# Values of four streams in three tiles, outputs a pair later and new orders in a chain of attention layers

## The reference

```python
xn = rmsnorm(x, norm_w)
q, k, v = xn @ wq, cond @ wk, cond @ wv
attn = softmax(einsum('btgrd,bsgd->bgrts', qg, k) / sqrt(8))
x = x + (einsum('bgrts,bsgd->btgrd', attn, v) @ wo)
q, k, v = x @ Wq, ctx @ Wk, ctx @ Wv
probs = softmax(q @ k.T / 8 + col_bias)
x = (probs @ v) @ Wo + bo + x
```

## Time and profile before

| | |
|---|---|
| median of 3 runs | 2015.4 us |
| the profiled execution: time, span | 2012.08 us, 2010.3 us |
| mean granted TensorE clock | 0.973 |
| busy: TensorE, VectorE, GpSimd, ScalarE | 94%, 83%, 75%, 72% |
| DMA queue 1 | 1,164,412 packets, 305.43 MB, 81.1% of 16 engines |
| chain that ended last | PE 63%, DMA 11%, POOL 9%, issue 6%, SPq 4%, DVE 4%, ACT 2% |

### The profile page before, as it was taken

One profiled execution on the slowest core, in us unless ns is written; L12 is line 12 of the kernel. 1 busy time (PEld: TensorE's weight loads), 2 busy tenths in 40 slices (PEclk: granted clock), 3 DMA queues, 4 the chain that ended last, 5 costly groups with the idle time before them and its releaser, 6 DMA issues.

```text
span 2010.3 us, 76315 instructions
## 1 busy us (share of the span) xinstructions
PE 1886.1 (94%) x28784; PEld 1570.3 (78%) x28784; DVE 1672.3 (83%) x3516; ACT 1443.4 (72%) x2603; POOL 1497.9 (75%) x1830
## 2 busy tenths in 40 slices
PE   5699999999899998999999999999989999999995
PEld 5578887788788887888778887888878788888874
DVE  7588888898788887888788888889878888898873
ACT  3377777777677776777677777777767777777762
POOL 2478777787687876788777887778767787788862
PEclk7599999999999999999999999999999999999997
DMA  4278888989889899898888888888887888787884
GB/s 157 55 141 161 160 160 159 166 159 159 150 162 163 156 166 148 164 165 155 161 152 167 159 156 154 171 162 159 157 151 161 161 159 159 154 162 162 162 149 102
DMA packets 1164823, 310.79 MB, mean 155 GB/s; under 512 B 1139254, under 2 KB 1163132, under 8 KB 1164412
## 3 DMA queue, kind: packets, MB, share of 16 engines
q1 hardware_dynamic: 1164412, 305.43, 81.1%
HBM read 15.93 MB, written 4.19 MB: 10 GB/s over the span
## 4 chain that ended last, share of the span: by engine, by line
PE 63%; DMA 11%; POOL 9%; issue 6%; SPq 4%; DVE 4%; ACT 2%; POOLq 0%; ACTq 0%; DVEq 0%
PE ring L1129 35%; DMA arena<-arena 10%; PE sc L1262 6%; PE o_ps L1129 6%; PE ring L1331 4%; PE o_ps L1280 3%; POOL arena L589 3%; PE sc L1245 2%; PE sc L1260 2%; POOL p_sm L566 2%; DMA arena<-p_sm 2%; SPq L443 2%; POOL v_packed L584 1%; POOL p_sg L561 1%; PE ring L1200 1%
## 5 line engine op out<-in xcount | busy, mean ns | idle before, releaser
L561 POOL TENSOR_TENSOR p_sg<-arena,p_sg 128x512 f16<-128x512 f32 (+1 forms) x256 | 347.5, 1357 | 205.9 <-ACT p_sg L626 205.9
L1129 PE MATMUL ring<-ctx_two,m_w 128*128 128x154 f16 x6144 | 442.8, 232 | 2.2 <-DVE o_tg L818 2.2
L1129 PEld LDWEIGHTS ring<-ctx_two,m_w 128*128 128x128 f16 x6144 | 426.2, 98 | 3.2 <-DVE o_tg L818 3.1
L1001 DVE TENSOR_TENSOR arena<-sc,row_max 128x616 f32<-128x616 f32 (+2 forms) x512 | 405.7, 793 | 17.4
L566 POOL TENSOR_TENSOR p_sm<-arena,p_sm 128x616 f16<-128x616 f32 x256 | 337.6, 1319 | 99.7 <-ACT p_sm L626 99.7
L1129 PE MATMUL ring<-wv_m,ctx_two 128*77 128x512 f16 x1536 | 363.1, 381 | 1.0 <-DVE q_mix L822 1.0
L626 ACT ACTIVATE arena<-ring 128x462 f16<-128x462 f32 (+1 forms) x384 | 196.6, 512 | 141.7 <-PE ring L1129 141.7
L589 POOL TENSOR_TENSOR arena<-arena 128x1024 f16<-128x1024 f32 x128 | 272.9, 2132 | 29.1 <-ACT arena L626 25.4
L1129 PEld LDWEIGHTS ring<-wv_m,ctx_two 128*77 128x77 f16 x1536 | 165.2, 116 | 149.1 <-DVE q_mix L822 46.6
L1262 PE MATMUL sc<-arena,x_s 128*128 128x512 f16 (+1 forms) x1152 | 263.4, 337 | 0.0
L720 ACT ACTIVATE arena<-arena,log_w,rstd 128x512 f32<-128x512 f32 (+1 forms) x256 | 227.4, 888 | 9.2 <-DVE arena L1001 9.2
(11 more groups left out here) (160 smaller groups left out, 3611.6 us busy)
## 6 DMA issues: line engine op xcount, KB each, us to landing
ctx_nat<-in_ctx_dram SPq DMA_DIRECT2D x64, 77.0 KB
x_nat<-in_x_dram SPq DMA_DIRECT2D x64, 64.0 KB, 2.9
arena<-p_sg SPq DMA_TRANSPOSE x256, 3.3
arena<-p_sm SPq DMA_TRANSPOSE x256, 3.9
out_dram<-y_out SPq DMA_DIRECT2D x64, 64.0 KB, 2.2
arena<-in_L_xattn_Wk_dram SPq DMA_DIRECT2D x2, 1024.0 KB, 6.0
arena<-in_L_xattn_Wv_dram SPq DMA_DIRECT2D x2, 1024.0 KB, 6.5
arena<-arena SPq DMA_TRANSPOSE x128, 4.7
```

The source lines that it names most:

```text
L561: pool.tensor_tensor(p_sg[k][:, LO, 0:e - a], probs_flat[:, a:e], p_sg[k][:, HI, 0:e - a], ALU.subtract).then_inc(sems["pg_lo"], 1)
L1001: dve.tensor_tensor(shifted[:, hs, :], s_view[:, hs, :], row_max[:, hs].unsqueeze(2).to_broadcast([P, hs.stop - hs.start, S]), ALU.subtrac ...
L1129: ins = pe.matmul(out, a, b, start=(n == 0), stop=(n == len(passes) - 1))
```

## The change

- **Values.** The 77 rows of the fourth stream of each four (stream 3 or 7, "part 3") are cut into pieces of 26, 26 and 25. `ctx_four` has room for 26 more context columns behind each stream's 77, and `context_parts` (GpSimd) copies the pieces there. `context_values` of the first three streams makes 103 or 102 rows at once; part 3 runs no `context_values` and no `values` on ScalarE or VectorE. Its rows are copied from the three tiles into `v_fourth` by SP (`move_values`, one DMA per stream), and `values_m` of part 3 waits for them.
- **GQA output product.** `wo_g` and `o_tg` are fp32: ScalarE copies the turned outputs once (`turned`), `low_turned` goes, and `output_g` is one fp32 matmul.
- **Maxima.** Two parts, heads 0 to 12 and 13 to 15, in place of 6, 7 and 3; the first waits for the second score bank.
- **Outputs.** `turn_out(m - 4)`, `output_m(m - 6)` and `finish_m` or `last_layer(m - 6)` take the place of m - 2 and m - 4: one pair later.
- **Orders.** SP and TensorE are in the diff. GpSimd: `x_parts(g+2)`, `inverse_norm`, `low_part(g)` twice, `spread_keys`, `pack_values`, `context_parts`, `x_parts(m+2)`, `low_part(m, 0)`, `low_out`, `low_part(m, 1)`. ScalarE: `folded` three times, `exponential_g` 0, `turn_context`, `high_g` 0, `exponential_g` 1, `last_layer`, `high_g` 1, `keys_values`, `queries`, `picked_values`, `exponential_m` 0, `high_m` 0, `values` 0, `turned`, `high_out`, `values` 1, `exponential_m` 1, `high_m` 1. VectorE: `maximum_g`, `folded` 0 and 1, `shift_g` 0, `first_x`, `folded` 2, `shift_g` 1, `turn_context`, `normalise_g`, `finish_m`, `finish_g`, `maximum_m` 0, `shift_m` 0, `keys_values`, `queries`, `normalise_m` twice, `maximum_m` 1, `shift_m` 1, `values` twice.

The diff, without the counts of semaphores and the lists of GpSimd, ScalarE and VectorE:

```diff
-    MAX_PARTS = list(zip((0, BANK // S, 2 * BANK // S), (BANK // S, 2 * BANK // S, H)))
+    MAX_PARTS = [(0, 2 * BANK // S), (2 * BANK // S, H)]
...
+    PART = -(-S // 3)
+    PART_OF = [(i * PART, min(S, (i + 1) * PART)) for i in range(3)]
+    def part(m):
+        return stream(m) % 4
+    def rows(m):
+        a, e = PART_OF[part(m)]
+        return S + e - a
+    def same_tile_before(m):
+        return m - (8 if part(m) == 1 else 4)
+    def split_stream(m):
+        return m - PLACES[layer(m)] + 2 * (3 - part(m))
...
-        uses = [("g", lead, k) for k in chunks] + [("yg", g - 4, 0), ("ct", g + 4, 0), ("ym", m - 4, 0), ("kv", g + 2, 0)]
-        return uses + [("vp", g, 0), ("q", g + 2, 0), ("ot", g - 2, 0), ("v", m, 0), ("v", m, 1)]
+        return [("g", lead, chunks[0]), ("g", lead, chunks[1]), ("g", lead, chunks[2]), ("ct", g + 4, 0), ("ym", m - 6, 0),
+                ("yg", g - 4, 0), ("kv", g + 2, 0), ("vp", g, 0), ("q", g + 2, 0), ("ot", g - 2, 0),
+                ("v", m, 0), ("v", m, 1)]
...
-        ctx_two = [sb(f"ctx_two{n}", [P, 2, KC, 2, S], F16) for n in range(STREAMS // 2)]
-        ctx_t = [ctx_two[n // 2][:, :, :, n % 2, :] for n in range(STREAMS)]
+        ctx_four = [sb(f"ctx_four{n}", [P, 2, KC, 4, S + PART], F16) for n in range(STREAMS // 4)]
+        ctx_t = [ctx_four[n // 4][:, :, :, n % 4, 0:S] for n in range(STREAMS)]
...
-        v_mha = [sb(f"v_mha{n}", [P, 2, H, MD + 1], F16) for n in range(2)]
+        v_tile = [sb(f"v_tile{n}", [P, 2, H, MD + 1], F16) for n in range(2)]
+        v_fourth = sb("v_fourth", [P, 2, H, MD + 1], F16)
+        v_mha = [v_tile[0], v_tile[1], v_tile[0], v_fourth]
...
+            def move_values(it, m):
+                a, e = PART_OF[part(m)]
+                sp.wait_ge(sems["v_lo"], at("v_lo", it, m, 2))
+                sp.nop(nofuse=True)
+                fourth = m - 2 * (part(m) + 1)
+                if exists(it, fourth):
+                    sp.wait_ge(sems["om_raw"], at("om_raw", it, fourth, 2))
+                    sp.nop(nofuse=True)
+                moved = m - (2 if part(m) else 4)
+                if exists(it, moved):
+                    sp.wait_ge(sems["v_moved"], at("v_moved", it, moved, 16))
+                    sp.nop(nofuse=True)
+                sp.dma_start(v_fourth[a:e].rearrange("p a h d -> p (a h d)"),
+                             v_mha[part(m)][S:S + e - a].rearrange("p a h d -> p (a h d)")).then_inc(sems["v_moved"], 16)
...
             def pair(it, n):
+                if exists(it, m - 2) and part(m - 2) != 3:
+                    move_values(it, m - 2)
+                if exists(it, m - 4):
+                    turn_out(it, m - 4)
                 if exists(it, g):
                     turn_g(it, g, 0)
                     turn_g(it, g, 1)
+                if layer(g + 4) == 0 and exists(it, g + 4) and exists(it + 1, g + 4):
+                    load(it, g + 4)
+                if layer(m - 6) == LAYERS - 1 and exists(it, m - 6):
+                    store(it, m - 6)
                 if exists(it, m):
                     turn_m(it, m, 0)
-                if layer(m - 4) == LAYERS - 1 and exists(it, m - 4):
-                    store(it, m - 4)
-                if layer(g + 4) == 0 and exists(it, g + 4) and exists(it + 1, g + 4):
-                    load(it, g + 4)
-                if exists(it, m - 2):
-                    turn_out(it, m - 2)
-                if exists(it, m):
...
+            def context_parts(it, g):
+                c = ctx_four[stream(g) // 4]
+                pool.wait_ge(sems["ct_lo"], at("ct_lo", it, g, 1))
+                for n, (a, e) in enumerate(PART_OF):
+                    piece = c[:, :, :, 3, a:e].rearrange("p a k s -> p (a k) s")
+                    ins = pool.tensor_tensor(c[:, :, :, n, S:S + e - a].rearrange("p a k s -> p (a k) s"), piece,
+                                             ones_h[:, :].unsqueeze(2).to_broadcast([P, 2 * KC, e - a]), ALU.mult)
+                ins.then_inc(sems["ct_parts"], 1)
...
             def values(it, n, m, k):
-                if k == 0 and exists(it, m - 4):
-                    act.wait_ge(sems["om_raw"], at("om_raw", it, m - 4, 2))
-                high(v_mha[m // 2 % 2][0:S, HI, n0 // MD:n1 // MD, 0:MD], ring[0:S, b, :].rearrange("p (h d) -> p h d", d=MD),
+                before, r = same_tile_before(m), rows(m)
+                if k == 0 and exists(it, before):
+                    act.wait_ge(sems["om_raw"], at("om_raw", it, before, 2))
+                    act.wait_ge(sems["v_moved"], at("v_moved", it, before, 16))
+                high(v_mha[part(m)][0:r, HI, n0 // MD:n1 // MD, 0:MD], ring[0:r, b, :].rearrange("p (h d) -> p h d", d=MD),
...
-            def high_turned(it, n, g):
+            def turned(it, n, g):
...
-                high(o_tg[:, HI, :], ring[:, b, 0:T], 1.0).then_inc(sems["ot_hi"], 1)
+                high(o_tg[:, :], ring[:, b, 0:T], 1.0).then_inc(sems["ot_copy"], 1)
...
             def maximum_m(it, m, k):
-                dve.wait_ge(sems["sm_raw"], at("sm_raw", it, m, k + 1))
+                dve.wait_ge(sems["sm_raw"], at("sm_raw", it, m, k + 2))
...
-            def low_turned(it, n, g):
-                b = ring_bank(n, ("ot", g, 0))
-                dve.wait_ge(sems["ot_hi"], at("ot_hi", it, g, 1))
-                low(o_tg[:, LO, :], ring[:, b, 0:T], 1.0, o_tg[:, HI, :]).then_inc(sems["ot_lo"], 1)
...
             def folded(it, n, m, k):
-                ct, w, b, (h0, h1) = ctx_two[stream(m) // 2], layer(m) // 2, bank_for(it, n, ("g", m, k)), G_CHUNKS[k]
+                two = slice(stream(m) % 4, stream(m) % 4 + 2)
+                ct, w, b, (h0, h1) = ctx_four[stream(m) // 4], layer(m) // 2, bank_for(it, n, ("g", m, k)), G_CHUNKS[k]
...
-                    ins = split_product(ring[:, b, (h - h0) * 2 * S:(h - h0 + 1) * 2 * S],
+                    ins = split_product(ring[:, b, (h - h0) * 2 * S:(h - h0 + 1) * 2 * S].rearrange("p (t s) -> p t s", t=2),
...
-                                          hl(lambda i: ct[:, i, kc].rearrange("p t s -> p (t s)"))) for kc in range(KC)])
+                                          hl(lambda i: ct[:, i, kc, two, 0:S])) for kc in range(KC)])
...
             def context_values(it, n, m, k):
-                ct, w, b, (n0, n1) = ctx_t[stream(m)], layer(m) // 2, bank_for(it, n, ("v", m, k)), V_CHUNKS[k]
-                split_product(ring[0:S, b, :],
-                              [(hl(lambda i: ct[:, i, kc, :]), hl(lambda i: wv_m[w][:, i, kc, n0:n1])) for kc in range(KC)]).then_inc(sems["v_raw"], 1)
+                w, b, (n0, n1), r = layer(m) // 2, bank_for(it, n, ("v", m, k)), V_CHUNKS[k], rows(m)
+                ct = ctx_four[stream(m) // 4][:, :, :, part(m), :]
+                if k == 0:
+                    pe.wait_ge(sems["ct_parts"], at("ct_parts", it, split_stream(m), 1))
+                split_product(ring[0:r, b, :],
+                              [(hl(lambda i: ct[:, i, kc, 0:r]), hl(lambda i: wv_m[w][:, i, kc, n0:n1])) for kc in range(KC)]).then_inc(sems["v_raw"], 1)
...
-                pe.wait_ge(sems["v_lo"], at("v_lo", it, m, 2))
+                if part(m) != 3:
+                    pe.wait_ge(sems["v_lo"], at("v_lo", it, m, 2))
+                else:
+                    pe.wait_ge(sems["v_moved"], at("v_moved", it, m - 2, 16))
...
-                                            [(hl(lambda i: p_tm[:, k, i, h - k * HALF, :]), hl(lambda i: v_mha[m // 2 % 2][:, i, h, :]))])
+                                            [(hl(lambda i: p_tm[:, k, i, h - k * HALF, :]), hl(lambda i: v_mha[part(m)][:, i, h, :]))])
...
             def output_g(it, n, g):
-                pe.wait_ge(sems["ot_lo"], at("ot_lo", it, g, 1))
-                split_product(ring[:, b, 0:T], [(hl(lambda i: wo_g[w][:, i, :]), hl(lambda i: o_tg[:, i, :]))]).then_inc(sems["yg_raw"], 1)
+                pe.wait_ge(sems["ot_copy"], at("ot_copy", it, g, 1))
+                pe.matmul(ring[:, b, 0:T], wo_g[w][:, :], o_tg[:, :], start=True, stop=True).then_inc(sems["yg_raw"], 1)
...
             def pair(it, n):
+                if exists(it, lead):
+                    folded(it, n, lead, chunks[0])
                 if exists(it, g):
                     scores_g(it, g)
                 if exists(it, lead):
-                    folded(it, n, lead, chunks[0])
                     folded(it, n, lead, chunks[1])
                     folded(it, n, lead, chunks[2])
                 if exists(it, g - 2):
                     values_g(it, g - 2)
+                if layer(g + 4) == 0 and exists(it, g + 4):
+                    turn_inputs(it, n, g + 4)
+                if exists(it, m - 6):
+                    output_m(it, n, m - 6)
                 if exists(it, m):
                     scores_m(it, m, 0)
                 if exists(it, g - 4):
                     output_g(it, n, g - 4)
-                if layer(g + 4) == 0 and exists(it, g + 4):
-                    turn_inputs(it, n, g + 4)
```

(11 more changed lines are left out.)

113 lines of the change are left out of this document (60 added, 53 removed).

## The result

The changed kernel took 2045.3 us (median of 4 runs, 2033.5 to 2052.0), the kernel before 2014.0 beside it (4 runs, 2012.3 to 2023.8): ratio 1.0138, interval 1.0088 to 1.0188. That is slower, where 1958 us was forecast, and outside the range of 1889 to 2004. The profiled execution took 2033.5 us, so 12 us less than the median.

What follows compares the result with a forecast made beforehand. The prediction took TensorE to bound quiet pairs (13.94 us), with stalls of 12.1 us a round, mostly for transposed outputs. Its terms summed as 2012.1 + 5 - 13 - 46 = 1958 us, range 1889 to 2004.

Steps and rivals of the forecast that it cites:

- Outputs one pair later, -46: `turn_out` issued a pair earlier than it is read: TensorE's wait in `output_m` goes, 46 us less, bounds 0 and -59.
- Output product in fp32, +5: `output_g`: one fp32 matmul for three fp16 adds 0.05 us a pair, 5 us in 96 pairs, up to 9.
- Maxima in two parts, slack in VectorE (rival 4): VectorE starts 1.1 us later, after the second score bank; in a normal pair 0.9 us of slack covers it.
- rival 4: VectorE's loop becomes the bound in every pair, slower: 2051 us at a path of 14.6 us; chance 0.10.
- the turn of the loop: Between rounds: a 2.9 us gap without releaser, 4.7 us a round with its pair and slow matmuls.
- Part-3 pairs at 13.5 instead of 13.94, -13: Pairs without values are bound by the path to the turned outputs' copy: 0.4 us shorter, 32 times, 13 us less.
- rival 2: The clock falls in each part-3 pair's gap: 1.25 us, 32 times, +40, giving 1998 us; chance 0.14.
- the row at 547.52: TensorE wait in the earlier trace, cited against rival 2: after 2.26 us idle, 24 matmuls took 1.50 us.
- the rule of the Trainium skill: On TensorE's clock: short matmul bursts with idle waits between let it fall each time; by it, 1998 us.
- Rival 3: Output wait only replaced, by `turn_m` held behind the moved transpose and the values copy: 2004 us; chance 0.09.
- The forecast's case: Whole kernel: three of four quiet pairs at 14.0 us, one at 13.5, `output_m` wait gone: 1958 us; chance 0.52.

Runs made afterwards that it cites:

- e15_late_early_product: Kernel before with outputs one pair later, their transpose first in the queue's list, `output_m` ahead of the first MHA scores, two `o_s`: 1974.7 us, ratio 0.9783.
- e2_four_values: Changed kernel with the sharing undone, all four streams making their own values by matmuls: 1976.2 us, ratio 0.9798.
- e10_four_two_os: Changed kernel with all four streams' values made by matmuls and two `o_s` buffers: 1974.9 us, ratio 0.9802.
- e11_filled_two_os_no_copy: Changed kernel with unread matmuls filling the part-3 gap, two `o_s` and no copies of values (streams 3 and 7 left out): 1980.9 us, ratio 0.9821.
- e4_norm_first: Changed kernel with GpSimd's `inverse_norm` ahead of `x_parts(g+2)` again, as before the change: 2038.5 us, ratio 1.0120.
- e3_no_copy: Changed kernel without `move_values` and the waits for it, values of streams 3 and 7 left out: 2019.8 us, ratio 1.0011.
- e1_two_os: Changed kernel with two `o_s` buffers in turn for the output's parts: 2029.0 us, ratio 1.0066.
- e9_filled_two_os: Changed kernel with six unread matmuls in the part-3 pairs and two `o_s` buffers: 2005.5 us, ratio 0.9950.

## Why the prediction was wrong

**Outputs one pair later, -46.** Right: -44 in `e15_late_early_product`. That it is right rests on `output_m` being moved ahead of the scores, which the prediction used ("may start when `output_m` of the pair has freed `o_t`") but did not price; with `output_m` left where it was, the kernel took 158 us more with the transpose at the head of the list, and 571 more with it at the end and two `o_s`.

**Output product in fp32, +5.** Right in size by TensorE's busy time in `output_g`: 49.3 us for 128 items in `e2_four_values`, against 42.3 before, so 0.055 each and 7 in all. In the time it does not show (1974.9 and 1974.7 us for `e10_four_two_os`, which has it, and `e15_late_early_product`, which has not), and the length of a pair does not give it either: a quiet pair takes 14.03 us with it and 13.93 before, but in the looped rounds of `e15_late_early_product`, with the old product, it takes 14.03 too.

**Maxima in two parts, slack in VectorE (rival 4).** Right that it is covered: nearly all pairs of `e2_four_values` take 14.0 to 14.6 us, with TensorE busy throughout, except those about the turn of the loop.

**Part-3 pairs at 13.5 instead of 13.94, -13.** This is the step that failed: the sharing, put at -13 us, measured +69 (3.40 points, `e2_four_values`). The path of the pair itself was read rightly: with the three disturbances away, the quiet part-3 pair of each looped round takes 13.49 us (`e11_filled_two_os_no_copy`), and in the changed kernel TensorE stands idle for 1.90 in front of the folded product (2.2 forecast), released by ScalarE's `o_tg`. But there only the last of the eight rounds has 13.49 at this place. The step costed the pair by that one path, let the next pair be a quiet one, and put the clock, the queue and the buffers at nothing. In fact the two together take 1.3 to 2.8 us more than forecast, in the looped rounds mostly in the first, in the last round in the second. Three prices were missing:
- *The clock behind the gap*, 1.06 points, 21 us. This was rival 2, at +40 and 0.14. Its mechanism holds: filling the gap with unread matmuls removes the falls and the time. Its size was off, since it had the clock fall in all 32 pairs, at 1.25 us each; it fell behind 13 of 31 gaps, at 1.6 us (14, 22 and 23 in `e4_norm_first`, `e3_no_copy` and `e1_two_os`, with gaps as long). The forecast set the row at 547.52 against it (2.26 us idle, clock kept); that row was one draw of a thing that goes either way. The prediction took the rule of the Trainium skill (page "TensorE: Matmul & The Clock Gate", section "HAM oscillation — how this bites in real kernels") to mean a fall in every part-3 pair. The page's case is another one: there each burst of matmuls is shorter than the wait behind it, and here a gap of 1.90 us stands behind some 11.5 us of matmuls. The traces alone decide, with a fall behind some of the gaps.
- *The one `o_s`*, 0.72 points, 15 us. No rival had it. With `turn_out` of an item issued a pair later, `o_s` is held until then, and the next `high_out` waits for that transpose, 52 times. The prediction asked what frees `o_t`, which `turn_out` writes, and never what `turn_out` reads and from then on holds longer. The later `turn_out` alone doesn't bring the wait: without copies it is 4.6 us (`e3_no_copy`) and without the sharing 3.0 (`e2_four_values`), against 58.2. It is a second price of the copies.
- *The copies*, 1.27 points, 26 us. The step said "anything from nothing to the longest landing seen, 6.32 us, is hidden". That counts when the copy lands and it was true; no wait of TensorE in the changed kernel is put down to `v_fourth`. It left out what is queued behind: "I cost the queue at nothing, and it would cost about 1 us where a transpose is held up". Rival 3 had this wait, at the price of the output's gain and a chance of 0.09; the output's gain was kept and the wait came on top.

Together 3.17 points by `e11_filled_two_os_no_copy`, 64 us. From the forecast's 1958 to the measured 2045 are 87.

**The rest, 23 us,** is still in `e11_filled_two_os_no_copy` (1981 against 1958). A quiet part-3 pair is 13.49 us there and the pair behind it 14.03, as forecast:

```profile
1831.88:1845.37 13.49, 12.88 (x216) 11.03 (x216) 11.55 (x23) 10.09 (x18) 11.19 (x15) 1.00 1.04 167
1845.37:1859.40 14.03, 14.03 (x224) 12.02 (x223) 11.90 (x24) 10.75 (x20) 11.74 (x15) 1.00 1.09 155
```

What is longer is the turn of the loop. Its gap without releaser, 2.92 us before in the turn of the earlier trace rows, is in this kernel (total of 5 turns, longest 6.7):

```profile
PE ring L1188 <- issue: 29.6, 5, 6.7
```

5.9 us a turn, where the kernel before has 14.3 us in five: 15 us more. The forecast had carried the turn over unchanged. In the changed kernel it is two gaps a turn, 21.1 us in all. The remaining 8 us or so are not accounted for; among them, not every part-3 pair of this kernel gains: the four of a looped round take 14.57, 14.40, 13.49 and 14.05 us in the mean, against 14.59, 14.31, 14.01 and 14.55 with four values products (`e2_four_values`). Why the gap grows is open: the profile names no releaser, and no run was made for it. It is short where pairs are full of work (16.0 in `e2_four_values`) and in `e9_filled_two_os`, so neither the new order of the program nor the filling alone explains it.

**The chances.** The forecast's case had 0.52 and its gain of 57 us consisted for four fifths of a term that came true. The range ended at 2004 because each rival was counted alone: rivals 2 and 3 both came true in part, in the part-3 pairs and those behind them, beside a cost that no rival listed. Their common root, a queue and two engines with little slack around a pair made irregular, was one case that needed a chance of its own on the slow side.

## What to carry to other kernels

When a change makes every fourth pass of a pipeline lighter, the pass may gain little, and it and the next one can lose more: cost both, with each transfer and buffer that the irregular pass holds. For a step moved later ask two things, what it writes and what it reads and now keeps. And for an added DMA ask first what is issued behind it, not when it lands; here the later output brought from -44 to +571 us by where its transpose and its product were put.
